# A graph network on one core: matrix strips gathered inside the counting walk, scores kept per node in layers 2 and 3

## The reference, cut to what matters

```
h = maximum(layernorm(x), 0)
# layer 2 (layer 3 alike, with slope 0.01, no W, another output function)
hW = h @ W
s_src, s_dst = hW @ a_src, hW @ a_dst
e = leaky_relu(s_src[src] + s_dst[dst], 0.2)
m = segment_max(e, dst)
ex = exp(e - m[dst])
out = segment_sum(ex / segment_sum(ex, dst)[dst] * hW[src], dst) + b
x = x + leaky_relu(out, 0.3)
```

## Time and profile before

| | |
|---|---|
| median of 3 runs | 4647.93 us (4639.51 to 4649.34) |
| profiled execution, its own time | 4662.39 us |
| its span | 4660.6 us |
| PE, VectorE, ScalarE, GpSimd busy | 71%, 83%, 46%, 40% of the span |
| mean granted clock of TensorE | 0.885 of full speed |
| DMA traffic | 674.29 MB, 145 GB/s over the span |

### The profile page before, as it was taken

How to read it: one execution, slowest core, us unless ns; L and a number is a source line. 1 busy time by engine, 2 the same in 40 slices (tenths; PEclk the granted TensorE clock), 3 DMA queues, 4 the chain that set the end, 5 groups by cost and what they waited for, 6 DMA issues and landing times. The chain is left out here.

```text
span 4660.6 us, 66751 instructions
## 1 busy us (share of the span) xinstructions
PE 3310.9 (71%) x20061; PEld 1474.2 (32%) x20061; DVE 3863.6 (83%) x6856; ACT 2147.7 (46%) x4394; POOL 1851.4 (40%) x3682
## 2 busy tenths in 40 slices
PE   5555552026639999999991699999999994166156
PEld 2111111001214444444440344444444442022122
DVE  8999993369968888898888788888888883897898
ACT  6999980047613343343340344444443431075075
POOL 0000006710057777677670466666666663000000
PEclk9999995557869999999995799999999996588589
DMA  4653339976535555555550233333333331544444
GB/s 171 256 208 141 148 142 295 362 254 211 164 83 140 148 142 143 143 142 140 146 141 12 64 91 94 91 94 91 94 91 94 91 94 56 172 176 168 172 152 171
DMA packets 359859, 674.29 MB, mean 145 GB/s; under 512 B 71068, under 2 KB 261724, under 8 KB 347856
## 3 DMA queue, kind: packets, MB, share of 16 engines
q1 hardware_dynamic: 319824, 591.23, 38.6%
q0 software_dynamic: 39680, 78.78, 6.4%
HBM read 398.98 MB, written 270.79 MB: 144 GB/s over the span
## 5 line engine op out<-in xcount | busy, mean ns | idle before, releaser
L670 POOL DMA_INDIRECT arena<-h_table,gidx x808 | 782.6, 969 | 314.6 <-issue 229.7
L818 PE MATMUL banks<-arena,lw 128*65 128x512 f32 (+3 forms) x1050 | 460.6, 595 | 260.8 <-DVE lw L1517 134.3
L1625 DVE TENSOR_TENSOR arena<-banks,arena 128x512 f32<-128x512 f32 x808 | 536.3, 685 | 61.5 <-PE banks L857 43.2
L767 PE MATMUL banks<-arena 128*128 128x500 bf16 x1440 | 366.2, 376 | 278.3 <-DVE arena L1359 271.9
L1745 DVE TENSOR_TENSOR arena<-banks,arena 128x512 f32<-128x512 f32 x808 | 518.8, 684 | 36.6 <-PE banks L967 13.1
L1753 DVE TENSOR_TENSOR arena<-banks,arena 128x512 f32<-128x512 f32 x808 | 516.7, 681 | 1.3 <-PE banks L973 1.3
L1091 ACT ACTIVATE arena<-arena 128x128 bf16<-128x128 f16 x1440 | 455.6, 390 | 40.8 <-DVEq L1290 40.8
L636 POOL DMA_INDIRECT arena<-slots,slot_i x157 | 168.4, 1073 | 746.1 <-DMA slots<-arena 690.2
L1226 ACT ACTIVATE arena<-banks 64x256 f32<-64x256 f32 x808 | 305.8, 378 | 341.2 <-PE banks L999 334.2
L987 PE MATMUL banks<-arena 128*64 128x256 f32 x3232 | 438.5, 392 | 0.5 <-DVE arena L1755 0.5
L973 PE MATMUL banks<-arena 64*128 64x512 f32 x1616 | 436.2, 617 | 1.2 <-DVE arena L1753 0.9
(11 more groups left out here) (287 smaller groups left out, 6329.2 us busy)
## 6 DMA issues: line engine op xcount, KB each, us to landing
arena<-c_flat SPq DMA_DIRECT2D x75, 1562.5 KB, 6.8
slots<-arena SPq DMA_DIRECT2D x90, 1000.0 KB, 3.9
arena<-hs_dump SPq DMA_DIRECT2D x404, 128.0 KB
arena<-mask_rows SPq DMA_DIRECT2D x50, 781.2 KB, 4.3
arena<-in_edge_attr SPq DMA_DIRECT2D x202, 128.0 KB
arena<-placed SPq DMA_DIRECT2D x202, 128.0 KB
xs_dump<-arena SPq DMA_DIRECT2D x202, 128.0 KB
hs_dump<-arena SPq DMA_DIRECT2D x202, 128.0 KB
```

The lines of the kernel that those rows point to most:

```text
L670: pool.indirect_dma_start(out=xs[par][:, k * D:(k + 1) * D], out_offset=None, in_=h_table, in_offset=bass.IndirectOffsetOnAxis(ap=gidx[par ...
L767: last = pe.matmul(ps[4 + r % 2][:, 0:BW], row_hot[r][:, k * P:(k + 1) * P], col_hot[r][:, k * BW:(k + 1) * BW], start=k == 0, stop=k == K ...
L818: last = pe.matmul(ps[j][0:rows, 0:n], lw[par][:, 0:rows], ptile[par][:, j * COLS:j * COLS + n], start=isinstance(b, int) and b == 0, stop ...
L1625: V.tensor_tensor(bt[j], ps[5 + j % 2][:, :], h2k[t % 2], ALU.mult).then_inc(bt_sb, 1)
```

## The change

Two things are changed.

- The walk and the relayout. A panel is now 12 strips (13 panels, the last of 13 strips). `slots` is laid out by step, then partition, so that the first steps' strips are complete in DRAM while the walk goes on. GpSimd gathers panel g as soon as flush 53 + 3g has landed and panel g-2 has been copied. VectorE copies panels 0 to 7 inside the walk, one half after the `total` of step 230 + 17g and the other one step later; SP stores them right after the flush that ends at or behind that step. Panels 8 to 12 follow behind the walk: 8 at once, 9 after the first rows are found, 10 before the node stage, 11 and 12 after it. The 25 row searches come after the last gather. Buffers are moved in SBUF to make room.
- Layers 2 and 3. The other end's score is not spread over all partitions any more. It is used per node (`other_of`), before the maxima are spread, and two rows are spread in place of one. The feature copy `lw` is gone: PE takes the features and a column of ones straight from `proj`. Of `big_m` only the last 75 columns are cleared, and the first block's maximum is a plain subtraction.

The diff, cut to its core:

```diff
...
-WIDE = 16
+WIDE = 12
+PANELS = WN // WIDE
+INSIDE = 8
...
-    slots = nc.dram_tensor("slots", (P * SL, BW), F32).ap()
-    slots_v = slots.rearrange("(p s) f -> p s f", p=P)
+    slots = nc.dram_tensor("slots", (SL * P, BW), F32).ap()
+    slots_v = slots.rearrange("(s p) f -> p s f", p=P)
...
+        def panel(g):
...
+            lo = g * WIDE
+            n = WIDE if g < PANELS - 1 else WN - lo
+            return lo, n, (GN - 1 + lo + n - 1) // 4
...
+        def copied_after(g):
...
+            return 230 + 17 * g
...
+            def store_panel(g):
...
+                lo, n, _ = panel(g)
+                cols = min(n * WD, N - lo * WD)
+                for half, (b, nb) in enumerate(((0, 13), (13, 12))):
+                    sp.wait_ge(relaid_sb, 2 * g + half + 1)
+                    sp.dma_start(c_cols[:, b:b + nb, lo * WD:lo * WD + cols],
+                                 relaid[half][:, 0:nb * n * WD].rearrange("p (b f) -> p b f", b=nb)[:, :, 0:cols]).then_inc(relaid_out[half], 16)
...
+                    for g in range(INSIDE):
+                        if (copied_after(g) + 1) // 4 == i * 2 + par:
+                            store_panel(g)
...
-            for i in range(-(-WN // WIDE)):
-                n = min(WIDE * WD, N - i * WIDE * WD)
-                for half, (lo, nb) in enumerate(((0, 13), (13, 12))):
-                    sp.wait_ge(relaid_sb, 2 * i + half + 1)
-                    sp.dma_start(c_cols[:, lo:lo + nb, i * WIDE * WD:i * WIDE * WD + n],
-                                 relaid[half][:, 0:nb * WIDE * WD].rearrange("p (b f) -> p b f", b=nb)[:, :, 0:n]).then_inc(relaid_out[half], 16)
+            for g in range(INSIDE, PANELS):
+                store_panel(g)
...
-                sp.wait_ge(relaid_out[half], 16 * -(-WN // WIDE))
+                sp.wait_ge(relaid_out[half], 16 * PANELS)
...
-            for par in range(2):
-                pool.wait_ge(flushed[par], 16 * (SL // 8))
-            pool.wait_ge(placed_zeroed, 16 * -(-W * D // CROW))
-            pool.wait_ge(table_out, 16)
-            for i in range(-(-WN // WIDE)):
-                if i >= 2:
-                    pool.wait_ge(relaid_sb, 2 * i - 2)
-                for w in range(i * WIDE, min(i * WIDE + WIDE, WN)):
-                    pool.indirect_dma_start(out=win[i % 2][:, (w % WIDE) * BW:(w % WIDE + 1) * BW], out_offset=None, in_=slots,
-                                            in_offset=bass.IndirectOffsetOnAxis(ap=slot_i[:, w:w + 1], axis=0)).then_inc(win_in[i % 2], 16)
-                if i == 1:
-                    pool.wait_ge(rows_ready, 1)
-                for b in range(3 * i - 3, min(3 * i, NB)) if i else ():
+            def gather_panel(g):
...
+                lo, n, q = panel(g)
+                pool.wait_ge(flushed[0], 16 * (q // 2 + 1))
+                pool.wait_ge(flushed[1], 16 * ((q + 1) // 2))
+                if g >= 2:
+                    pool.wait_ge(relaid_sb, 2 * g - 2)
+                for w in range(lo, lo + n):
+                    pool.indirect_dma_start(out=win[g % 2][:, (w - lo) * BW:(w - lo + 1) * BW], out_offset=None, in_=slots[0:(q + 1) * 4 * P, :],
+                                            in_offset=bass.IndirectOffsetOnAxis(ap=slot_i[:, w:w + 1], axis=0)).then_inc(win_in[g % 2], 16)
...
+            def find_rows(lo, hi):
...
+                for b in range(lo, hi):
...
+            for g in range(PANELS):
+                gather_panel(g)
+            pool.wait_ge(placed_zeroed, 16 * -(-W * D // CROW))
+            pool.wait_ge(table_out, 16)
+            pool.wait_ge(rows_ready, 1)
+            find_rows(0, NB)
...
-                        last = pe.matmul(ps[j][0:rows, 0:n], lw[par][:, 0:rows], ptile[par][:, j * COLS:j * COLS + n],
+                        last = pe.matmul(ps[j][0:rows, 0:n], proj[:, b, 2:rows + 2] if base else lw[par][:, :], ptile[par][:, j * COLS:j * COLS + n],
...
+            def copy_panel(g, half):
...
+                lo, n, _ = panel(g)
+                dve.wait_ge(win_in[g % 2], 16 * (WIDE * (g // 2) + n))
+                if g:
+                    dve.wait_ge(relaid_out[half], 16 * g)
+                w4 = win[g % 2][:, 0:n * BW].rearrange("p (w b d) -> p b w d", w=n, b=NB)
+                b, nb = ((0, 13), (13, 12))[half]
+                o4 = relaid[half][:, 0:nb * n * WD].rearrange("p (b w d) -> p b w d", b=nb, w=n)
+                V.tensor_copy(out=o4, in_=w4[:, b:b + nb, :, :]).then_inc(relaid_sb, 1)
...
+            copies = {copied_after(g) + half: (g, half) for g in range(INSIDE) for half in range(2)}
+            assert max(copies) < SL
...
                     total(i * 8 + (8 + j), j, i * 16 + 16)
+                    if i * 8 + 8 + j in copies:
+                        copy_panel(*copies[i * 8 + 8 + j])
             for s in range(SL - 8, SL):
...
                 total(s, s % 8, 16 * (SL // 8 - 1))
+                if s in copies:
+                    copy_panel(*copies[s])
+            for half in range(2):
+                copy_panel(INSIDE, half)
...
-                    V.tensor_copy(out=proj[:, 7 * g:7 * g + n, :], in_=ps[g][:, 0:n * (D + 2)].rearrange("p (b f) -> p b f", b=n)).then_inc(proj_sb, 1)
+                    V.tensor_copy(out=proj[:, 7 * g:7 * g + n, 0:D + 2], in_=ps[g][:, 0:n * (D + 2)].rearrange("p (b f) -> p b f", b=n)).then_inc(proj_sb, 1)
...
-                dve.wait_ge(brow_sb, NJ * (k + 1))
...
+            for half in range(2):
+                copy_panel(INSIDE + 2, half)
...
-            for i in range(-(-WN // WIDE)):
-                n = min(WIDE, WN - i * WIDE)
-                dve.wait_ge(win_in[i % 2], 16 * (WIDE * (i // 2) + n))
-                w4 = win[i % 2].rearrange("p (w b d) -> p b w d", w=WIDE, b=NB)
-                for half, (lo, nb) in enumerate(((0, 13), (13, 12))):
-                    if i:
-                        dve.wait_ge(relaid_out[half], 16 * i)
-                    o4 = relaid[half][:, 0:nb * WIDE * WD].rearrange("p (b w d) -> p b w d", b=nb, w=WIDE)
-                    V.tensor_copy(out=o4[:, :, 0:n, :], in_=w4[:, lo:lo + nb, 0:n, :]).then_inc(relaid_sb, 1)
-                for b in range(3 * i - 3, min(3 * i, NB)) if i else ():
-                    dve.wait_ge(row_found[b % 3], 16 * (b // 3 + 1))
-                    at(row_counted, b, dve)
-                    V.scalar_tensor_tensor(junk_b, found[b % 3], nid[:, b:b + 1], ones[:, 0:1].to_broadcast([P, W]),
-                                           ALU.is_le, ALU.mult, accum_out=cnt_in[:, b:b + 1]).then_inc(row_counted, 1)
+            for g in range(INSIDE + 3, PANELS):
+                for half in range(2):
+                    copy_panel(g, half)
+            dve.wait_ge(brow_sb, NJ)
+            for b in range(NB):
+                dve.wait_ge(row_found[b % 3], 16 * (b // 3 + 1))
+                at(row_counted, b, dve)
+                V.scalar_tensor_tensor(junk_b, found[b % 3], nid[:, b:b + 1], ones[:, 0:1].to_broadcast([P, W]),
+                                       ALU.is_le, ALU.mult, accum_out=cnt_in[:, b:b + 1]).then_inc(row_counted, 1)
...
-                ran(V.memset(big_m, -BIG))
-                settle()
...
-                def score(b):
-                    return proj[:, bass.ds(b, 1), D:D + 1].rearrange("p b f -> p (b f)")
+                ran(V.memset(big_m[:, N:NP], -BIG))
...
-                    V.scalar_tensor_tensor(big_m[:, 0:N], mask4[r], score(b), big_m[:, 0:N], ALU.subtract, ALU.max,
-                                           reverse0=True).then_inc(maxed, 1)
...
-                largest(0, 0, 0, 0)
-                each(1, NB, largest)
+                    if b == 0:
+                        V.tensor_scalar(big_m[:, 0:N], mask4[r], proj[:, b, 0:1], -1.0, ALU.subtract, ALU.mult).then_inc(maxed, 1)
+                    else:
+                        V.scalar_tensor_tensor(big_m[:, 0:N], mask4[r], proj[:, b, 0:1], big_m[:, 0:N], ALU.subtract, ALU.max,
+                                               reverse0=True).then_inc(maxed, 1)
...
+                each(0, NB, largest)
+                settle()
...
-                for j in range(NJ):
+                dve.wait_ge(mt_sb, NJ * (k + 1))
+                do(V.tensor_tensor(stat[:, 0, :], mxt[:, :], other_of, ALU.add))
+                do(V.scalar_tensor_tensor(stat[:, 1, :], stat[:, 0, :], slope, stat[:, 0, :], ALU.mult, ALU.max))
+                ran(V.tensor_tensor(stat[:, 2, :], other_of, stat[:, 1, :], ALU.subtract))
+                ran(V.scalar_tensor_tensor(stat[:, 3, :], other_of, slope, stat[:, 1, :], ALU.mult, ALU.subtract))
+                ran(V.tensor_scalar(slope_score[:, :], score_of, slope, None, ALU.mult))
+                settle()
+                for i in range(2 * NJ):
+                    j = i % NJ
...
-                    dve.wait_ge(mt_sb, NJ * k + j + 1)
-                    V.tensor_tensor(m_row[:, 4 * j * P:(4 * j + n) * P].rearrange("p (b n) -> p b n", b=n),
```

(14 more changed lines are left out.)

103 lines of the change are left out of this document (57 added, 46 removed).

## The result

| | kernel before | changed kernel |
|---|---|---|
| time, median of 4 runs | 4645.12 us (4639.51 to 4649.34) | 4572.5 us (4569.34 to 4585.21) |
| profiled execution, its span | 4662.39, 4660.6 us | 4585.21, 4583.4 us |
| last step of the walk ends | 685.9 us | 787.3 us |
| first load behind the stage's barrier | 975.1 us | 944.7 us |
| layer 2; layer 3 to the end | 361.4; 369.4 us | 336.8; 347.7 us |

The ratio is 0.985 (95% interval 0.9826 to 0.9873); the forecast was 4591 us, 4510 to 4660. The medians are 72.6 us apart. The 77.2 us between the two profiled executions are: walk +101.4, rest of the stage -131.8, layers 0 and 1 together -0.6, layer 2 -24.6, layer 3 -21.6.

What follows compares the result with a forecast made beforehand. The prediction took ScalarE and VectorE, both full, to bound the walk. Walk +131, behind it -137, layers 2 and 3 -51 make -57 us, applied to the 4647.93 us median: 4591 us, range 4510 to 4660.

Steps and rivals of the forecast that it cites:

- The copies: Walk: eight panels' copies on VectorE, 3.4 us for 13 blocks and 1.7 for 12, add 40.8 us.
- The slack: Walk from step 230: VectorE's spare 0.022 us a step gives back 2.8 us over 130 steps.
- The gathers' hits: Walk: 108 gathers meeting VectorE's work cost it 0.07 us each, 7.6 us in all (0 to 15).
- Rival C: Walk: gathers run only while VectorE waits, 56 us more, 4647 us; chance 0.05.
- The wait for flushes: Walk: VectorE waits 12 us for a flush behind a panel's store, seven times, adding 84 us (42 to 140).
- the sum: Walk: flush, store with its gathers, next flush and latency, 2.9 + 20 + 2.9 + 1.4, land after 27.2 us.
- The rule on ring order: SP's queue: each DMA engine consumes a queue's descriptors in order, so the 84 us of flush waits belong in the forecast.
- Rival A: Walk: engines interleave stores and flushes, so no flush is waited for, 84 us less, 4507 us; chance 0.15.
- Rival B: Walk and after: small packets make a store take 25.4 us and each wait 20; 4675 us, slower; chance 0.15.
- Behind the walk: Walk's end (T) to the barrier: last copy by T+99, counts done at T+152 instead of T+289, saving 137 us.
- Layers 2 and 3: Each layer saves 25.8 us: 14.1 before the maxima, 1.7 first maximum, 7.6 before the first score, 2.4 feature copy; 51 together.
- the first panel: Walk: panel 0's gathers land some 28 us after step 215, its copy stands 26.8 us on; adds 1 us.

Runs made afterwards that it cites:

- e5: Changed kernel, but gathers of a panel inside the walk wait until the stores of the panel two before have landed; ratio 0.9761 to the kernel before.
- e7: Changed kernel with each panel's second half copied eight steps after the first and gathers held until stores have landed; ratio 0.9756 to the kernel before.
- e9: The changed kernel measured again, unaltered, on another occasion; median 4576.77 us, ratio 0.9837 to the kernel before.
- e2: Kernel before with only the change's part for layers 2 and 3, old walk and gathers; 4600.89 against 4652.52 us, ratio 0.9888.
- e1: Changed kernel, but stores of panels 0 to 7 issued from ScalarE's queue, seven steps behind their copy; ratio 0.9781 to the kernel before.
- e12: Changed kernel with each panel's second half copied and stored eight steps after the first, gathers not held; ratio 0.9719 to the kernel before.
- e4: Changed kernel, but copied tiles have a row pitch of 260 numbers in place of 240, leaving gaps; ratio 0.9808 to the kernel before.

## Why the prediction was right, and where it was off

The time lay inside the range, 18.5 us under the 4591; the mechanism was right in part.

**The copies** were priced right: 40.8 forecast, 40.4 measured; the slow rate for an unbroken output of 13 blocks was the right choice of the two rows.

**The slack** was mis-sized: 0.022 us a step, from the difference of busy times. The sums of the changed kernel (L1409), first at 119 us, where ScalarE sets the pace, then behind a copy, where VectorE does:

```profile
119.77 0.73 DVE L1409 SCALAR_TENSOR_TENSOR arena<-arena,banks 128x500 f32<-128x500 f32 x1
120.42 1.12 DVE L1397 TENSOR_SCALAR arena<-arena,agg 128x500 bf16<-128x500 f16 x4
121.55 0.73 DVE L1409 SCALAR_TENSOR_TENSOR arena<-arena,banks 128x500 f32<-128x500 f32 x1
```

```profile
470.35 0.72 DVE L1409 SCALAR_TENSOR_TENSOR arena<-arena,banks 128x500 f32<-128x500 f32 x1
470.99 1.12 DVE L1397 TENSOR_SCALAR arena<-arena,agg 128x500 bf16<-128x500 f16 x4
472.03 0.72 DVE L1409 SCALAR_TENSOR_TENSOR arena<-arena,banks 128x500 f32<-128x500 f32 x1
```

1.78 against 1.68 us: 0.10 a step, at most 13 us over the 130 steps, where I had 2.8. At 470 us the sum starts at 472.03, before the comparisons end (472.11); at 121 us it starts at 121.55, just after their end (121.54). So a VectorE that is behind overlaps its instructions more, and one that is not looks as busy while it has slack. The balance agrees: 40.4 + 72.0 - 101.4 = 11.0 us recovered in the change, and in e5 to e7 it is about 12 by the same sum with all their waits.

**The gathers' hits** were mis-sized too: 7.6 us forecast. The comparisons took 345 ns on average as before, and 407.0 us in all against 404.8. GpSimd's issues between 430 and 787 us took 1107 ns on average, 1.41 us with the 0.30 of issue, where my upper bound was 1.95, and no copy inside the walk waited for them. Rival C, gathers kept out, is refuted.

**The wait for flushes** came in the form and number forecast, seven times, 10.3 us in place of 12, 72 in place of 84. Counted from the flush before the store, the flush that was waited for landed after 24.5 to 26.6 us; the sum had 27.2. But the step that explained it, "A flush issued behind a panel's store must therefore wait for the whole store", holds for a sixth to a third of it: without that order 60.1 us stay, 49.6 of them at the same seven panels. The sum came out near because it counted store, gathers and flushes one after the other, and that is what the engines' load asks for on any queue: the right number, in good part for another reason. The rule on ring order that I weighed fits the trace (each flush behind a store landed 2.1 to 5.1 us after it), but it is not the main cause. Rival A (no waits, 4507 us) fell, and its premise with it: interleaved streams share the engines and do not spare the wait.

**Rival B** needed 25.4 us for a store and 20 us for a wait; the longest was 11.7 (12.2 in e9).

**Behind the walk** the last copy was forecast at T + 99 and came at T + 99.6. The counts took 54.2 us in place of 46, as the fourth waited 8.76 us for a search that ran beside the last store; the stage ended at T + 157.4, not T + 152. The before is not sharp to a microsecond either: e2 ran the same instructions there from the walk's end to the first load in 284 us, the kernel before in 289.2.

**Layers 2 and 3** gave 46.2 us in this pair of executions, not 51 (e2 gave 50.2 by its trace and 51.6 by its medians). In layer 2 the start of the maxima came 14.2 us earlier (14.1 forecast), the first maximum took 1.77 us (1.8), the first score came 6.8 us earlier by the sums' part (7.6: TensorE took 12.47 us for its 14 sums, not 11.2) and the rest gave 1.9 (2.4). Layer 3 lacked 3 us more, by the granted clock in its projections.

Against the forecast sum of -57 us: the waits cost 12 us less than forecast, slack, hits and the first panel together 17 less, the rest of the stage gave back 5 less, layers 2 and 3 gave 5 less, and layers 0 and 1 took 0.6 less. That makes up the 20 us to 77.2.

## What to carry to other kernels

When a transfer is waited for, add up all that its DMA engines have to move between its issue and its landing, on every queue, before blaming the order on its own queue; a second queue bought 12 of 72 us (22 over the same seven panels), the same transfers spread over time 54. Move work in small pieces into a stage whose DMA engines have room, and look at the DMA share of that stretch, not only at the engines. Slack between two full engines is read from the interval of one engine's repeated instruction when it is behind, not from the difference of busy times.

## What was new about the hardware

- A flush on a queue of its own, with gathers and stores on two others, still kept VectorE waiting up to 10.5 us (e1); one issued at 543.08 us freed it 17.1 us later.
- SyncE's issue of a flush took 0.36 us in the median, but up to 10.27 us in the change, where stores of 3 MB stood before it, and never more than 0.36 in e12.
- A float32 copy of 13 blocks took 3.39 us into one run and 1.90 us into a tile with gaps, the same 3120 numbers; nothing but the pitch differs (e4).
- Some fifty matmuls of one layer's projections ran at a granted clock of 0.65 in one execution and 0.85 in another, 3 us apart; the change itself had the faster ones in neither layer in one execution and in layer 2 in the next (e9).
